# Two-layer MetaFormer: the job list's wait moved, layer 1's list made ahead of the gates, empty slots loaded with 16 columns

## What is computed

```python
# layer 0: hidden widths 432 528 624 752 896 1088 1312 1584
gate = softmax(x @ router_W.T); topk_val, topk_idx = top_k(gate, 2)
out += w_e * (silu(x @ gates[e].T) * (x @ ups[e].T) @ downs[e].T)      # for each e
# layer 1: hidden width 768, the two gates divided by their sum
out += tok_w[:, e] * (relu(x @ w1[e].T + b1[e]) @ w2[e].T + b2[e])     # for each e
```

## Time and profile before

| | us |
|---|---|
| median of three runs (215.5 to 216.11) | 215.62 |
| the profiled execution, its own time | 214.29 |
| its span | 212.5 |

### The profile page before, as it was taken

One profiled execution on the slowest core, in us unless ns is written; L12 is line 12 of the kernel. 1 busy time (PEld: TensorE's weight loads), 2 busy tenths in 40 slices (PEclk: granted clock), 3 DMA queues, 4 the chain that ended last, 5 costly groups with the idle time before them and its releaser, 6 DMA issues.

```text
span 212.5 us, 4269 instructions
## 1 busy us (share of the span) xinstructions
PE 189.1 (89%) x1656; PEld 130.0 (61%) x1656; DVE 99.9 (47%) x302; ACT 63.3 (30%) x144; POOL 32.0 (15%) x65
## 2 busy tenths in 40 slices
PE   7899899998969999999999688888996999990992
PEld 7679777567426656765558577555862567570471
DVE  0342787747732222354313239785695474440131
ACT  2243587627112222231132245883320000000000
POOL 1413400001891000000000012000139300000000
PEclk9999999999979999999999999999998899997698
DMA  6999999995000019999301999991000899996001
GB/s 211 425 437 409 414 457 401 432 384 181 21 3 0 0 29 364 401 420 424 147 3 24 350 405 414 427 419 54 0 3 0 270 369 352 356 355 231 0 3 45
DMA packets 7388, 51.21 MB, mean 241 GB/s; under 512 B 888, under 2 KB 2368, under 8 KB 3136
## 3 DMA queue, kind: packets, MB, share of 16 engines
q1 hardware_dynamic: 6784, 50.05, 59.8%
q10 hardware_dynamic: 576, 0.79, 1.2%
HBM read 50.64 MB, written 0.20 MB: 239 GB/s over the span
## 4 chain that ended last, share of the span: by engine, by line
PE 70%; DMA 11%; DVE 9%; issue 5%; ACT 3%; SPq 1%; POOL 1%; DVEq 0%; POOLq 0%
PE bank L1375 10%; DMA w<-bias_rows_dram 9%; PE bank L1454 7%; PE bank L1196 5%; PE bank L1078 5%; PE bank L1402 4%; PE bank L1151 4%; PE bank L1441 3%; PE bank L1330 3%; PE bank L1359 3%; PE bank L1208 3%; PE bank L1415 3%; PE bank L1110 3%; PE bank L1180 3%; PE bank L1309 2%
## 5 line engine op out<-in xcount | busy, mean ns | idle before, releaser
L1375 PE MATMUL bank<-w,scratch 128*64 128x512 f32 (+3 forms) x112 | 23.3, 547 | 3.1 <-DVE job_regs L939 3.1
L1078 PE MATMUL bank<-ones 128*128 128x128 f32 x162 | 23.6, 299 | 2.0 <-POOL ones L526 1.4
L1078 PEld LDWEIGHTS bank<-ones 128*128 128x128 f32 x162 | 21.7, 210 | 2.9 <-POOL ones L526 1.4
L685 ACT ACTIVATE scratch<-bank,neg_max 128x256 f32<-128x256 f32 x48 | 19.7, 480 | 7.8 <-DVE neg_max L810 7.6
L1454 PE MATMUL bank<-w,scratch 128*64 128x192 f32 x216 | 20.2, 332 | 0.0
L1454 PEld LDWEIGHTS bank<-w,scratch 128*64 128x64 f32 x216 | 14.4, 136 | 9.1 <-issue 4.8
L576 POOL TENSOR_SCALAR scratch<-const,place,gate 128x64 f32<-128x64 f32 x32 | 18.0, 579 | 5.4 <-issue 5.4
L534 POOL TENSOR_TENSOR rstd<-var_eps,minus_half 128x2 f32<-128x2 f32 x4 | 2.8, 710 | 101.5 <-DVE var_eps L747 101.5
L1196 PE MATMUL bank<-const,scratch 128*128 128x128 f32 x96 | 15.1, 284 | 2.5 <-ACT scratch L685 1.2
L810 DVE TENSOR_REDUCE neg_max<-bank 128x2 f32<-128x512 f32 x24 | 15.7, 681 | 3.2 <-PE bank L1180 3.2
L614 ACT ACTIVATE scratch<-bank 128x384 f32<-128x384 f32 x6 | 2.9, 491 | 44.3 <-PE bank L1424 44.3
(11 more groups left out here) (175 smaller groups left out, 280.9 us busy)
## 6 DMA issues: line engine op xcount, KB each, us to landing
w<-experts_dram SPq DMA_DIRECT2D x16, 1152.0 KB, 14.4
w<-items_dram SPq DMA_DIRECT2D x8, 1152.0 KB, 8.2
w<-experts_dram SPq DMA_DIRECT2D x1, 3624.0 KB, 13.7
w<-experts_dram SPq DMA_DIRECT2D x1, 3024.0 KB, 30.9
w<-experts_dram SPq DMA_DIRECT2D x1, 2496.0 KB, 20.1
w<-experts_dram SPq DMA_DIRECT2D x1, 2016.0 KB, 24.4
w<-experts_dram SPq DMA_DIRECT2D x1, 1704.0 KB, 40.2
w<-bias_slots_dram SPq DMA_DIRECT2D x1, 1536.0 KB
```

Of the source, the lines that this page charges most:

```text
L685: nc.scalar.activation(probs[:, h % HB, t, :], bank[h % HB][:, t * TOK:(t + 1) * TOK], ACT.Exp, bias=neg_max[:, h, t:t + 1]).then_inc(prob ...
L1078: nc.tensor.matmul(bank[b][:, 0:P], ones[:], ones[:], start=True, stop=True)
L1375: nc.tensor.matmul(first_bank(m, which)[rows, to:to + wide], xe_hi[:, e], w0[:, at:at + wide], start=col == 0, stop=False, tile_position=( ...
```

## The change

1. Layer 0: TensorE's wait for `jobs_ready` moves from the end of macro 0 to macro 1, between `first_lower` and `down`. Layer 1: it moves to macro 1, between `first_upper` and `turn_hidden`.
2. Both layers: the gather runs its four upper matmuls (`xn_hi`) first, then the four lower ones. The counting of candidates is two operations, not five; `cand_of` is computed in `list_slots`. `job_steps` and `job_number` become a function of their own, `number_macros`.
3. Layer 1: `count_candidates` comes ahead of `xn_lo` and `list_slots` ahead of the gates; TensorE makes the candidates' numbers between upper and lower gather matmuls, and the slots' sum right after the gather; `number_slots` comes right after the copy of `xe_lo`.
4. SP: the number of used slots, plus one, is written to `job_regs` (one more VectorE operation) and loaded (one more value load). For each slot SP compares and branches: a used slot is loaded as before, an unused one gets 16 of its columns (8 KB over 128 partitions).

```diff
         slot_of = carve_xnT(3 * items).rearrange("p (a k) -> p a k", a=3)
-        cand_count, cand_there, cand_at, job_steps, job_number = (carve_xnT(n) for n in (E + 1, 1, 2, max(JOB_MACROS), 1))
+        cand_count, cand_there, cand_at, job_steps, job_number = (carve_xnT(n) for n in (E, 1, 2, max(JOB_MACROS), 1))
         cand_of = carve_xnT(3)
...
         job_bias = carve_w0(2, HID1)
-        job_regs = ctx.enter_context(nc.sbuf_tensor("job_regs", [1, 1 + items], mybir.dt.int32))
+        job_regs = ctx.enter_context(nc.sbuf_tensor("job_regs", [1, 2 + items], mybir.dt.int32))
         count = sb("count", [E])
...
             def load_jobs(layer):
                 n = job_count(sp, layer)
+                more = sp.value_load(job_regs[0:1, 1 + ITEMS[layer]:2 + ITEMS[layer]], min_val=1, max_val=ITEMS[layer] + 1)
                 def load(k):
...
                                 sp.wait_ge(main[layer]["down_done"], free)
-                            of = (items0, experts1)[layer][:, bass.ds(item, 1), :].rearrange("p e c -> p (e c)")
-                            sp.dma_start(w0[:, at:at + ROOM], of).then_inc(job_landed[layer][k], 16)
+                            whole = (items0, experts1)[layer][:, bass.ds(item, 1), :].rearrange("p e c -> p (e c)")
+                            with sp.If(more > QUADS * k + q + 1):
+                                sp.dma_start(w0[:, at:at + ROOM], whole).then_inc(job_landed[layer][k], 16)
+                            with sp.Else():
+                                sp.dma_start(w0[:, at:at + 16], whole[:, 0:16]).then_inc(job_landed[layer][k], 16)
                             if layer == 1:
...
             def count_candidates(layer):
                 sems, cand = main[layer], candidates[:, layer]
-                step(nc.vector.tensor_copy(count[:], bank[4][:, TT * E:(TT + 1) * E]))
-                step(nc.vector.tensor_tensor(cand_count[:, 0:E], count[:], cand[:, 0:E], ALU.mult))
-                step(nc.vector.tensor_reduce(cand_count[:, E:E + 1], cand_count[:, 0:E], AX_X, ALU.add))
-                nc.vector.tensor_tensor(cand_there, cand_count[:, E:E + 1], cand[:, E:E + 1], ALU.is_gt).then_inc(sems["cand_ready"], 1)
+                step(nc.vector.scalar_tensor_tensor(cand_count, bank[4][:, TT * E:(TT + 1) * E], cand[:, E:E + 1], cand[:, 0:E],
+                                                    ALU.is_gt, ALU.mult))
+                nc.vector.tensor_reduce(cand_there, cand_count, AX_X, ALU.add).then_inc(sems["cand_ready"], 1)
+            def list_slots(layer):
+                sems, n = main[layer], ITEMS[layer]
                 dve.wait_ge(sems["cand_ready"], 1)
-                step(nc.vector.tensor_scalar(cand_of, cand[:, E + 1:E + 4], cand_there, None, ALU.mult))
-            def list_slots(layer):
-                sems, n = main[layer], ITEMS[layer]
+                done = tick(nc.vector.tensor_scalar(cand_of, candidates[:, layer, E + 1:E + 4], cand_there, None, ALU.mult))
                 dve.wait_ge(sems["cand_psum"], 1)
+                dve.wait_ge(vec_step, done)
                 step(nc.vector.tensor_scalar(cand_at, bank[6][:, 0:2], 1.0, None, ALU.add))
...
                                             ALU.is_equal, ALU.mult).then_inc(sems["slots_ready"], 1)
+            def number_macros(layer):
                 step(nc.vector.tensor_scalar(job_steps, const[:, C_STEPS:CONST_W], cand_at[:, 1:2], None, ALU.is_lt))
...
                 step(nc.vector.tensor_copy(job_regs[0:1, 0:1], job_number[0:1, :]))
+                step(nc.vector.tensor_copy(job_regs[0:1, 1 + n:2 + n], cand_at[0:1, 1:2]))
                 nc.vector.tensor_copy(job_regs[0:1, 1:1 + n], slot_of[0:1, 2, 0:n]).then_inc(sems["jobs_ready"], 1)
             def pick_job(layer, k):
...
                                             place[:, t].unsqueeze(2).to_broadcast([P, E, STRIP]), ALU.is_equal).then_inc(chosen_ready, 1)
+                if layer == 1:
+                    count_candidates(1)
                 nc.vector.tensor_tensor(xn_lo, xn[:], xn_hi.bitcast(F32), ALU.subtract).then_inc(xn_split, 1)
+                if layer == 1:
+                    list_slots(1)
                 gates(layer)
-                count_candidates(layer)
+                if layer == 0:
+                    count_candidates(0)
+                else:
+                    number_macros(1)
                 dve.wait_ge(xe_psum, 2 * layer + 2)
...
                 if layer == 1:
+                    number_slots(1)
                     dve.wait_ge(combT_psum, 1)
...
                     dve.wait_ge(bias_landed, 32)
-                list_slots(layer)
+                else:
+                    list_slots(0)
+                    number_macros(0)
                 iteration(layer, 0)
-                number_slots(layer)
+                if layer == 0:
+                    number_slots(0)
                 for m in range(1, MACROS[layer]):
...
-            def gather(out_ap, c, tokens, ready=None):
+            def gather(out_ap, c, tokens):
...
                     for t in range(TT):
-                        if ready is not None and i == 0:
-                            pe.wait_ge(chosen_ready, ready + t + 1)
-                        elif ready is not None:
-                            pe.wait_ge(xn_split, ready // TT + 1)
                         last = nc.tensor.matmul(out_ap, part[:, t, c * P:(c + 1) * P], tokens(t),
...
+            def number_candidates(layer):
+                sems = main[layer]
+                pe.wait_ge(sems["cand_ready"], 1)
+                nc.tensor.matmul(bank[6][:, 0:1], upper, cand_there, start=True, stop=True, skip_group_check=True)
+                nc.tensor.matmul(bank[6][:, 1:2], ones[:], cand_there, start=False, stop=True, skip_group_check=True).then_inc(sems["cand_psum"], 1)
+            def sum_slots(layer):
+                sems, n = main[layer], ITEMS[layer]
+                pe.wait_ge(sems["slots_ready"], 3)
+                out_ap = bank[6][:, 0:3 * n].rearrange("p (a k) -> p a k", a=3)
+                nc.tensor.matmul(out_ap, ones[:], cand_slots[:, :, 0:n], start=True, stop=True).then_inc(sems["slots_psum"], 1)
             def iteration(layer, m, prepared=None):
...
                 first_upper(layer, m)
-                if m == 0:
-                    pe.wait_ge(sems["cand_ready"], 1)
-                    nc.tensor.matmul(bank[6][:, 0:1], upper, cand_there, start=True, stop=True, skip_group_check=True)
-                    nc.tensor.matmul(bank[6][:, 1:2], ones[:], cand_there, start=False, stop=True, skip_group_check=True).then_inc(sems["cand_psum"], 1)
-                else:
+                if m == 0 and layer == 0:
+                    number_candidates(0)
+                if m == 1 and layer == 1:
+                    pe.wait_ge(sems["jobs_ready"], 1)
+                if m > 0:
                     turn_hidden(layer, m - 1)
...
                 first_lower(layer, m)
-                if m == 0:
-                    pe.wait_ge(sems["slots_ready"], 3)
-                    n = ITEMS[layer]
-                    out_ap = bank[6][:, 0:3 * n].rearrange("p (a k) -> p a k", a=3)
-                    nc.tensor.matmul(out_ap, ones[:], cand_slots[:, :, 0:n], start=True, stop=True).then_inc(sems["slots_psum"], 1)
+                if m == 0 and layer == 0:
+                    sum_slots(0)
+                if m == 1 and layer == 0:
                     pe.wait_ge(sems["jobs_ready"], 1)
-                else:
+                if m > 0:
                     down(layer, m - 1)
             def drain(layer, k):
...
             def experts(layer):
...
                 for c in range(2):
-                    gather(bank[2 + c][:], c, lambda t: chosen[:, t].rearrange("p e s -> p (e s)"), TT * layer).then_inc(xe_psum, 1)
+                    for t in range(TT):
+                        pe.wait_ge(chosen_ready, TT * layer + t + 1)
+                        nc.tensor.matmul(bank[2 + c][:], xn_hi[:, t, c * P:(c + 1) * P], chosen[:, t].rearrange("p e s -> p (e s)"),
+                                         start=t == 0, stop=False)
                 if layer == 1:
+                    number_candidates(1)
+                pe.wait_ge(xn_split, layer + 1)
+                for c in range(2):
+                    for t in range(TT):
+                        last = nc.tensor.matmul(bank[2 + c][:], xn_lo[:, t, c * P:(c + 1) * P], chosen[:, t].rearrange("p e s -> p (e s)"),
+                                                start=False, stop=t == TT - 1)
+                    last.then_inc(xe_psum, 1)
+                if layer == 1:
+                    sum_slots(1)
```

More of the change, by code:

```diff
@@ L914, in count_candidates @@
                 sems, cand = main[layer], candidates[:, layer]
-                step(nc.vector.tensor_copy(count[:], bank[4][:, TT * E:(TT + 1) * E]))
-                step(nc.vector.tensor_tensor(cand_count[:, 0:E], count[:], cand[:, 0:E], ALU.mult))
```

(10 more changed lines are left out.)

## The result

| | before | after |
|---|---|---|
| median | 215.56 | 208.25 |
| executions | 214.83 to 216.11 | 204.84, 207.81, 208.69, 208.77 |
| profiled execution, its own time | 214.29 | 208.77 |
| its span | 212.5 | 206.7 |

The ratio is 0.957, 95% interval 0.945 to 0.970. Where a kernel's executions lie far apart, its ratio can go by the faster ones alone; this one goes by 204.84 and 207.81, and the quotient of the medians is 0.966. A second measurement gave 0.966 (0.961 to 0.971), median 207.12. Predicted were 207.8 and a ratio of 0.964. In what follows line 1359 of before is 1374, 1375 is 1390, 1415 is 1430, 1424 is 1439 and 1497 is 1496.

The account below looks back on a forecast made before the run. TensorE was taken as the bound, with list stops that also lower its clock, and the item transfers in layer 1's tail. Gains of 3.1 (layer 0) and 4.7 (layer 1), 7.8 together, gave median 207.8; range 205.0 to 211.0.

Parts of the forecast that it names:

- Layer 0, 3.1: Second macro of layer 0: without TensorE's list stop, at full clock, it ends at 61.15, not 64.28; gain 3.1 us.
- Rival (a): Layer 0's second macro: the clock falls all the same, 1.73 becomes up to 3.4 us; 209.5, chance 0.12.
- Its slack, "0.3 lost at most": Layer 0's last item load: lands at 104.2 before its use at 104.66, so SP's branch delay loses 0.3 us at most.
- The head of layer 1: Layer 1's start: first macro 1.4 us later, list 2.4 earlier, TensorE 2.7 earlier at the end; contained in layer 1's 4.7.
- From `jobs_ready` to the first issue: SP in layer 1: 2.15 us instead of 1.40, through a value load of 0.6 and a branch of 0.1 to 0.2.
- The branch per slot: SP's compare and branch before each item load: 0.1 us per slot, bounds 0 and 0.4.
- rival (e): SP's branch sets the loads' pace, from 2.9 us per slot on: slower than before, 216.3 or more; chance 0.03.
- The stream: Layer 1's item loads, 31.6 us before: the small last load saves 3.4 less 0.3 for its 64 B pieces, so 3.1.
- The landing: Layer 1's last item load: arrives at 191.7 instead of 196.41, a gain of 4.7 us; TensorE still waits about 3.
- The sum: Whole kernel: 3.1 in layer 0 plus 4.7 in layer 1 is 7.8 off; profiled execution 206.5, median 207.8.
- What follows is unchanged, low clock included: After layer 1's last wait: everything runs as before, at the low clock, so the 4.7 us gain stays whole.
- Rival (b): Layer 1's last wait: shrunk under 2.5 us, it leaves the clock up; 1.9 us more gained, 205.9, chance 0.08.

Follow-up runs that it names:

- the fastest version: Changed kernel with layer 1's eighth slot load made small at build time (no value load or branch), plus nine unread matmuls before the last wait: 204.15, ratio 0.950.

## Why the prediction held, and where its terms were off

**Layer 0, 3.1.** Line 1430 starts at 60.92 where line 1415 started at 64.28; 0.19 of it lies before this stage: 3.2. The start of the second macro was said 59.4, it is 59.05, or 59.24 with that 0.19; its length 1.73, it is 1.87. Rival (a) didn't occur: the granted clock is 1.00 there in every profile but the one that put the wait back. Putting it back costs 4.3 in the median and 3.5 by the ratios, so the part is worth about what was said.

**Its slack, "0.3 lost at most".** Wrong as a bound. Line 1374 waited 1.5, 0.2, 1.0 and 0.9 for the last item in four of the six profiles with this SP code (not with the list wait put back or layer 1's list made late), 1.2 and 3.0 in the two with the late value load, and not at all in the three without the branch or in the kernel before. A part is the branch: item loads whose room is free follow each other every 1.39, before every 1.10, so the last issue moved forward by 3.0 where TensorE moved by 3.4. In the first, fifteen of the last load's sixteen shares were in by 100.70 and one at 102.27; window and row of the changed kernel:

```profile
100.70:102.40 1.70, 0.66 (x8) 0.29 (x4) 0.95 (x2) 0.57 (x1) 0.00 (x0) 1.00 0.05 16
```

DMA engines 5% busy, and the load not done: the late share, not the rate. The packets of that share follow each other without a gap from 100.20 on, and among them, from 100.89 to 101.20, lies an instruction packet of 8 KB; the data packet behind it took 0.73, the others 0.35. That explains 0.7 of the 1.6; why the engine was behind before isn't shown. The step took the time from issue to landing (9.2 in one profile) as a constant; it went to 10.7.

**The head of layer 1.** Laid on `place` (154.46 before, 153.88 after): list 2.8 earlier (said 2.4), first macro 0.8 later (1.4), TensorE at the last wait 3.2 earlier (2.7). Two terms carry most of the difference. VectorE had the candidates' numbers 0.2 sooner than reckoned (its wait was 0.34, not 0.5), and gates and list both stand behind that. And from the gates to the first macro 0.7 was reckoned, where the gates' transposes take 0.3. GpSimd's weights made nobody wait, as said.

**SP.** From `jobs_ready` to the first issue 2.04 (said 2.15), the value load 0.65 with its branch. The Trainium skill (DMA: Bandwidth & Descriptors, Latency and other measured facts) puts the floor of such a load at about 600 ns; the trace agrees, with value loads that start 0.57 and 0.65 apart. The branch per slot was sized 0.1; the interval went from 1.64 to 1.90, so 0.26, inside the bounds 0 to 0.4. In layer 1 it cost nothing that the trace shows, since the queue sets the pace there; rival (e) needed 2.9.

**The stream.** The small load was to save 3.1. Between the two profiles the stream went from 31.6 to 28.7, 2.9; undoing the skip alone gives 2.4, and with the same code's 28.0 to 29.6 it could be anything from 1.2 to 2.9. The 128 pieces of 64 B took 11 ns each, 0.1 over 16 engines, where I took 0.3. The Trainium skill (DMA: Bandwidth & Descriptors, Specifications) has them as read-modify-write; the trace shows no price for it. The landing was said 191.7; laid on `place` it is 5.0 earlier than before, against 4.7 said, and the last wait 3.5 against "about 3".

**What was missing: the clock.** The sum put 206.5 for the profiled execution; it took 208.8. The parts of it: 1.5 of the item wait, 1.2 for the fall in layer 1's attention (4.51 for 2.83, less 0.5 by which the stop behind it was shorter, 0.15 for 0.67), less 0.4 that the rest did better. "What follows is unchanged, low clock included" was the step that didn't hold in either direction. In the attention the clock fell in both profiles of the changed kernel, with the list wait put back and with the late value load, though nothing was edited there; in five others and in the kernel before it didn't (the two with sixteen matmuls left aside). TensorE's gap ahead of it doesn't tell them apart (1.37 and 1.56 where it fell, 1.36 before and 1.87 in the fastest version, where it didn't). Why it falls there stays open. Where it stayed up, its gain was mostly not the full 1.7: in four of the five others TensorE stood for 1.0 to 1.3 a little later, and went on 2.58 to 2.60 after the end of an instruction packet of 8 KB each time, which leaves 0.6 to 0.9. In five of the twelve profiles, the changed kernel's second profile among them, the clock also fell at about 25, in layer 0's attention, for 3.4 us. Executions of one kernel differ in this: with a mean clock of 1.000, so with no fall at all, the changed kernel took 204.84, with 0.981 it took 208.69. The median came near 207.8 because it lies between the two, in part by luck. Rival (b)'s outcome is certain for that one execution alone. Its condition, a wait under 2.5, isn't borne out: the clock stayed up with a wait of 2.4 and fell with one of 2.1.

## What to carry to other kernels

Price a stop at the head of a chain with the clock that it costs afterwards, and a wait at the end too: twelve unread matmuls in one of 3.2 to 3.5 us were worth 1.7 us. A decision at run time costs its value load once (0.65 here) on the path from list to first transfer, so it must save more than that on the queue; and its branch per slot (0.3) counts where a later load has little slack. Before reading a difference of 1 us between two profiles, look how far the same code scatters: the stream of layer 1 did so by 1.6. And after adding instructions or far jumps, even harmless ones, look for "issue" in the chain and for late transfers where the bulk loads run: five matmuls cost 6 to 7 us.

## What the runs showed that I had not expected

- TensorE stood 4.2 us for instructions when a 16 KB instruction packet fell among bulk loads that took 94% of the queues' time; that packet took 0.96 us, and the engine went on 1.55 after its end. In the ten profiles without that gap it went on 1.60 to 1.62 after such a packet's end.
- SP stood 5.2 us after a jump, with an instruction packet ending 1.1 before it went on.
- One DMA engine of sixteen finished a 1152 KB load 1.6 us after the others, with the queue otherwise empty; an instruction packet lay among its last data packets.
- Pieces of 64 B took 11 ns each, against some 350 ns for one of 9216 B: 5.8 against 26 B/ns, so small, but without a penalty that 128 of them could show.
